# Moving the steps of a depthwise convolution along the taps of a deformable convolution's schedule

## The reference, cut to what matters

```python
# block 0, per image: n = group norm of x
xh = conv1x1(n, w_in, b_in)                     # 64 -> 128 channels
kernels = (relu(mean(xh) @ kg_w1.T + kg_b1) @ kg_w2.T + kg_b2)   # 3x3 taps for each channel
y = depthwise_conv(xh, kernels)
x = x + conv1x1(y * tanh(softplus(y)), w_out, b_out)
# block 1: n = group norm of x
offset, mask = conv3x3(n, w_off), sigmoid(conv3x3(n, w_mask))
xd = sum over 9 taps k of bilinear_sample(n, place k moved by offset) * mask[k], times w_def[:, :, k]
z = conv1x1(concat(xd, offset, mask), w_1x1); batch norm; x = x + silu(z)
```

## Time and profile before

| | us |
|---|---|
| three runs, median (lowest, highest) | 5537.8 (5534.99, 5549.79) |
| the profiled execution | 5550.28 |
| its span, first to last instruction | 5548.3 |
| PE busy | 4469.9 (81%) |
| DVE busy | 4494.7 (81%) |
| ACT busy | 2602.9 (47%) |
| POOL busy | 4053.5 (73%) |

### The profile page before, as it was taken

One profiled execution on the slowest core, in us unless ns is written; L12 is line 12 of the kernel. 1 busy time (PEld: TensorE's weight loads), 2 busy tenths in 40 slices (PEclk: granted clock), 3 DMA queues, 4 the chain that ended last, 5 costly groups with the idle time before them and its releaser, 6 DMA issues.

```text
span 5548.3 us, 46071 instructions
## 1 busy us (share of the span) xinstructions
PE 4469.9 (81%) x14762; PEld 2004.9 (36%) x14762; DVE 4494.7 (81%) x5306; ACT 2602.9 (47%) x3591; POOL 4053.5 (73%) x4243
## 2 busy tenths in 40 slices
PE   7587887887878888788887878788788887888874
PEld 3233333433434333343333433333343343333331
DVE  5888969789797887978889798897978879788765
ACT  4354545445445454444544454454445444445321
POOL 2677777777777777777777777777777777777776
PEclk8688878788787887878888788787878878788896
DMA  4334344353534435344353443435344353433433
GB/s 117 92 118 134 106 132 122 120 132 106 143 106 132 123 112 140 105 131 122 115 137 104 133 123 120 131 105 140 112 130 123 108 143 104 131 116 115 122 108 100
DMA packets 279695, 667.35 MB, mean 120 GB/s; under 512 B 76447, under 2 KB 116762, under 8 KB 277210
## 3 DMA queue, kind: packets, MB, share of 16 engines
q0 software_dynamic: 203328, 555.49, 33.9%
q1 hardware_dynamic: 76128, 108.93, 7.9%
HBM read 610.00 MB, written 54.12 MB: 120 GB/s over the span
## 4 chain that ended last, share of the span: by engine, by line
PE 38%; DVE 27%; POOL 18%; issue 11%; ACT 4%; DMA 2%; DVEq 0%; ACTq 0%; SPq 0%; POOLq 0%
POOL gat L507 18%; PE yo_ps L776 12%; PE tap_ps L776 7%; DVE gat L1370 6%; PE z_ps L698 6%; DVE pairs L1349 5%; DVE conv_ps L1240 5%; DVE hat_s L1397 4%; PE tap_ps L692 3%; PE conv_ps L571 2%; DMA gat<-patch_table,ixu 2%; PE conv_ps L646 2%; PE conv_ps L590 1%; DVE uc L1247 1%; PE xh_ps L758 1%
## 5 line engine op out<-in xcount | busy, mean ns | idle before, releaser
L507 POOL DMA_INDIRECT gat<-patch_table,ixu x4236 | 4045.2, 955 | 1480.6 <-issue 1264.6
L1370 DVE TENSOR_TENSOR gat<-gat,wgt_ps 128x1024 f32<-128x1024 f32 x1059 | 1283.4, 1215 | 445.1 <-DMA gat<-patch_table,ixu 438.1
L1349 DVE TENSOR_REDUCE pairs<-gat 128x256 f32<-128x1024 f32 x1024 | 1239.5, 1210 | 0.0
L776 PE MATMUL yo_ps<-hat_s,hat_image 128*128 128x512 f32 x1860 | 1009.1, 697 | 7.4 <-issue 7.4
L776 PE MATMUL tap_ps<-hat_s,hat_image 128*128 128x512 f32 x1860 | 887.2, 626 | 0.0
L692 PE MATMUL tap_ps<-ident,pairs 128*128 128x128 f32 x2048 | 393.5, 324 | 569.7 <-DVE pairs L1349 569.7
L1040 ACT ACTIVATE val<-tap_ps 128x512 f32<-128x512 f32 x512 | 303.2, 592 | 1094.8 <-PE tap_ps L692 1094.7
L776 PEld LDWEIGHTS yo_ps<-hat_s,hat_image 128*128 128x128 f32 x1860 | 418.5, 233 | 604.5 <-issue 594.5
L1240 DVE SCALAR_TENSOR_TENSOR conv_ps<-xh,kb,conv_ps 128x1024 f32<-128x1024 f32 x480 | 617.4, 1286 | 12.7
L692 PEld LDWEIGHTS tap_ps<-ident,pairs 128*128 128x128 f32 x2048 | 271.8, 163 | 884.0 <-DVE pairs L1349 709.0
L776 PEld LDWEIGHTS tap_ps<-hat_s,hat_image 128*128 128x128 f32 x1860 | 357.4, 201 | 422.2 <-issue 410.1
(11 more groups left out here) (243 smaller groups left out, 4886.5 us busy)
## 6 DMA issues: line engine op xcount, KB each, us to landing
gat<-patch_table,ixu POOLq DMA_INDIRECT x4236, 2.7
xb<-in_x SPq DMA_DIRECT2D x31, 1024.0 KB, 10.4
patch_table<-rec SPq DMA_DIRECT2D x120, 256.0 KB, 2.3
hat_image<-patch_table SPq DMA_DIRECT2D x144, 128.0 KB
out<-n_z SPq DMA_DIRECT2D x128, 128.0 KB, 2.4
patch_table<-np SPq DMA_DIRECT2D x2, 1072.5 KB
patch_table<-gat SPq DMA_DIRECT2D x8, 256.0 KB, 2.2
patch_table<-rec SPq DMA_DIRECT2D x16, 96.0 KB
```

The costliest lines, as they stand in the source:

```text
L507: pool.indirect_dma_start(gat[:, k, t * 2 * REC:(t + 1) * 2 * REC], None, table_rows, bass.IndirectOffsetOnAxis(ixu[:, i, k, t:t + 1], 0)) ...
L776: m = pe.matmul(hat_sums[t % 2][:, :], hat_image[:, q // NCH % 2, i, t, :], hat_s[:, i, :], start=(i == 0), stop=(i == HI - 1))
L1349: dve.tensor_reduce(total, gat[:, k, :].rearrange("p (t x c h) -> p t c x h", t=TILES, x=2, h=2), mybir.AxisListType.XY, ALU.add).then_inc ...
L1370: dve.tensor_tensor(patch, patch, wk.rearrange("p (n h) -> p n h", h=2).unsqueeze(2).to_broadcast([128, TILES * 2, C, 2]), ALU.mult).then_ ...
```

## The change

In every image's chunks 0 to 3 the convolution's rows come one tap earlier, and so do exp, ln and tanh; `project` moves from the next chunk's unit 1 to the own chunk's end, and `residual` from unit 3 to unit 1. The last image has a hat in all its chunks. At the start, the offsets, pixels, indices and points of image 0's chunk 1 come ahead of `hidden(1)`, whose normalisation moves from DVE to ACT. Before tanh, and before the first offsets of an image, ACT loads the set of tables that holds Silu as well as Tanh.

```diff
-PLAN_FIRST = ((2, "convolve 0"), (3, "convolve 1"), (5, "convolve 2"), (6, "exp"), (7, "ln"), (8, "tanh"))
-PLAN_BLOCK0 = ((1, "project"), (3, "residual"), (3, "convolve 0"), (4, "convolve 1"), (5, "convolve 2"), (6, "exp"),
-               (7, "ln"), (8, "tanh"), (8, "finish"))
+PLAN_FIRST = ((1, "convolve 0"), (2, "convolve 1"), (4, "convolve 2"), (5, "exp"), (6, "ln"), (7, "tanh"), (KK, "project"))
+PLAN_BLOCK0 = ((1, "residual"), (2, "convolve 0"), (3, "convolve 1"), (4, "convolve 2"), (5, "exp"), (6, "ln"), (7, "tanh"), (8, "finish"), (KK, "project"))
 PLAN_START = (
...
+    ((2, "first_offsets 2"), (4, "first_offsets 3"), (5, "first_pixels 1"), (6, "first_offsets 4"), (6, "first_points 2"), (8, "first_offsets 5"),
+     (KK, "first_pixels 2")),
+    ((3, "first_offsets 6"), (4, "first_offsets 7"), (5, "first_pixels 3"), (6, "first_points 3")),
+    ((6, "first_points 4"),),
 )
-PLAN_NORM = ((1, "project"), (3, "residual"), (4, "group_mean"), (5, "group_var"), (6, "normalise"), (8, "finish"))
+PLAN_NORM = ((1, "residual"), (4, "group_mean"), (5, "group_var"), (6, "normalise"), (8, "finish"))
...
-    return q < B * NCH and q % NCH in (HATS if q >= NCH else HATS0)
+    return q < B * NCH and (q >= (B - 1) * NCH or q % NCH in (HATS if q >= NCH else HATS0))
...
+    if g < 4:
+        plan = PLAN_BLOCK0 if g > 0 else PLAN_FIRST
+        if b == 0 and g < len(PLAN_START):
+            plan = by_unit(plan, PLAN_START[g])
...
             first_table(7)
+            pe.wait_ge(rec_done, ACT_COPIES[NCH - 1] + REC0)
+            pe.wait_ge(rec_dve, len(BY_DVE))
+            offsets(0, 1, 1)
             x_mean(1)
             x_var(1)
+            first_pixels(0, 1)
             x_norm(1)
             hidden_units(1)
             kernels(1)
...
             for s in range(NCH // 2):
                 hidden(1, s)
-            offsets(0, 1, 1)
-            first_pixels(0, 1)
...
-                steps = {"project": lambda b, g, i: project(b + 1, g - 1),
+                steps = {"project": lambda b, g, i: project(b + 1, g),
...
-                if n > 1:
+                if n > 0:
                     if s == 0:
                         act.wait_ge(kernel_dve, n * KERNEL_STEPS + 7)
...
             def tanh(n, s, buf=0):
                 u = mish[buf]
                 if n > 0:
+                    act.preload_act_table_set("silu_and_others")
...
             def offsets_two(n, s):
 
+                if s == 0:
+                    act.preload_act_table_set("silu_and_others")
...
             x_norm(1)
+            first_points(1)
             kernels(1)
-            for s in range(NCH // 2):
-                hidden(1, s)
-            first_points(1)
```

More of the change, by code:

```diff
@@ L827, in _ @@
             kernels(1)
-            pe.wait_ge(rec_done, ACT_COPIES[NCH - 1] + REC0)
-            pe.wait_ge(rec_dve, len(BY_DVE))
             for s in range(NCH // 2):
                 hidden(1, s)
-            offsets(0, 1, 1)
-            first_pixels(0, 1)
             def image(b, more, further):
-                steps = {"project": lambda b, g, i: project(b + 1, g - 1),
+                steps = {"project": lambda b, g, i: project(b + 1, g),
                          "group_mean": lambda b, g, i: group_mean(b + 1), "group_var": lambda b, g, i: group_var(b + 1),
@@ L1110, in _ @@
             first_index(0)
+            offsets(0, 1, 1)
             x_var(1)
+            first_pixels(0, 1)
             x_norm(1)
             hidden_units(1)
+            first_index(1)
             for s in range(NCH // 2):
                 hidden(1, s)
-            offsets(0, 1, 1)
-            first_pixels(0, 1)
-            first_index(1)
             def image(b, more, further):
@@ L1482, in image @@
                 steps = {"convolve": lambda b, g, i: convolve(b + 1, g, i),
-                         "project": lambda b, g, i: project(b + 1, g - 1),
+                         "project": lambda b, g, i: project(b + 1, g),
                          "residual": lambda b, g, i: residual(b + 1, g - 1), "group_mean": lambda b, g, i: group_mean(b + 1),
```

## The result

The kernel became slower: 5674.9 us (5668.8 to 5682.7, four runs) against 5539.2 (5535.0 to 5549.8, four runs beside them), a ratio of 1.0241 [1.0226, 1.0257]. The forecast was 5680. The profiled execution took 5672.5 us, its span 5670.7.

The account below looks back on a forecast made before the run. POOL's gathers and its waits for the transposes bound the kernel. Profiled 5550.3 + 154 (waits, images 1 to 14) - 3 (image 0) - 11 (last image) = 5690, as a median about 5680 us; range 5590 to 5750.

Parts of the forecast that it names:

- The lever: On POOL, only the number of gathers, its start and its waits for the transposes change the time.
- forecast +154: POOL's added waits over images 1 to 14: +11.0 us an image, +154 us in all.
- The chunk as a chain: Chunks 1 to 3: tap 3 reduced at 26.1, PE's chain 17.3, DVE's end 3.9, so 47.3 us against 44.6.
- The first group: Transposes of the first two taps come about 1 us later, behind residual and first row on DVE; not in the sum.
- I take 17.1 again: PE's chain from group 1's transposes stays 17.1 us, with slow clock after idling, within 13.0 to about 17.8.
- rival C: PE stays at full clock, chain 13.0 us, +0.8 us an image: no change, 5535 us; chance 0.08.
- the bound of 13.0: PE's chain from group 1 at full clock takes 13.0 us, taken from chunk 4.
- the sign that the clock is 0.50 behind both idle stretches: PE idles before group 0 and group 1 in chunks 1 to 3, granted clock 0.50 after both.
- Chunk 0: Tap 3 reduced at 24.9 us; chunk 42.0 or 46.1 us by PE's chain, 43.5 taken, +2.9.
- The product: At the own chunk's end it runs inside DVE's stall, costing nothing; tanh ends near 40.8 us, ahead of 43.4.
- Tables: Silu's own load of 1.28 us goes in some 60 chunks; effect on the time 0.
- the sum (5690): Profiled 5550.3 us + 154 - 3 (image 0) - 11 (last image) = 5690 us.

Follow-up runs that it names:

- the first: Changed kernel with only the convolution's third row put back behind tap 3's reduction in chunks 0 to 3: 5490.3 us, ratio to the kernel before 0.9901.
- second experiment: Kernel before with only the convolution's third row moved ahead of tap 3's reduction: 5777.7 us in one run, against 5549.9.
- third experiment: Kernel before with only product and projection moved to the own chunk's end: 5528.3 us, ratio to the kernel before 0.9966.
- fourth experiment: Kernel before with only image 0's new order, the last image's hats and the Silu-Tanh table set: 5523.3 us, ratio 0.9958.
- sixth experiment: Changed kernel with residual and first row behind tap 1's reduction in chunks 1 to 3: 5674.5 us, ratio to the kernel before 1.0240.
- fifth experiment: Changed kernel plus useless matmuls on PE ahead of groups 0 and 1, chunks 0 to 3 of images 1 to 14: 5628.9 us in one run, against 5546.0.
- the last (5480.2 to 5446.9): Changed kernel, third row behind tap 3, residual and earlier rows behind tap 1 (5480.2 us), plus 8 useless matmuls before group 1: 5446.9 us, ratio 0.9830.

## Why the prediction was right

- **The lever.** Only the number of gathers, POOL's start and its waits for the transposes could change the time. They did: net of issue, the waits of images 1 to 14 went from 73.6 to 226 us, +152 (forecast +154); those of image 0 from 21.4 to 16.3, -5 (-3); the last image's eight gathers fewer are worth 8 x 1.254 = 10 (11). With the shorter gathers (-16, last point) and POOL's first gather (at 104.84 instead of 103.36 us) these make 122, the difference of the spans (5670.7 - 5548.3).
- **The chunk as a chain.** 26.1 + 17.3 + 3.9 = 47.3 was worked out, 26.05 + 17.4 + 3.9 = 47.3 was measured. The third row ahead of tap 3 is shown as the cause from both sides, by the first and the second experiment.
- **Luck in the sum.** That +154 and +152 agree to 2 us is better than the terms do. Over images 1 to 14 chunks 1 and 2 grew by 2.5 and 2.9 us on the mean, close to the 2.7 taken, but chunk 0 by 3.9 (39.9 to 43.8) where 2.9 was taken: 14 us more in all, if POOL waits for all of it as the prediction had it. Against this POOL's waits at tap 0 of chunk 5, 13.0 us net of issue over these images before, are gone after; the prediction counted nothing there for the product that chunk 4 loses. They are gone in the third experiment, which takes that product away too, and still 14.0 in the fourth, which leaves it.
- **The first group.** The second group's lateness sets the sum, so residual and first row ahead of tap 1 cost nothing beside it (sixth experiment). The prediction had counted the second group alone.
- **The clock.** The step "I take 17.1 again" held, and rival C fell: the stretch after 5.65 us of idle was granted 0.50. At full clock the chain measured 13.7 (fifth experiment); the bound of 13.0 was misread from chunk 4, whose chain has no mask matmuls. Of the sign that the clock is 0.50 behind both idle stretches only the half on group 1 came: the 5.8 us from group 0's transposes on (2677.20) were granted 0.69 on the mean. So the clock costs 3.4 us of each such chunk of 47.3; holding it brought 46 us in the fifth experiment (with chunk 0's loss in it) and 33 us, 0.6%, in the last (5480.2 to 5446.9). The Trainium skill (TensorE: Matmul & The Clock Gate, Part 1: The HAM clock gate) puts the ramp penalty at under 1% of a typical kernel's span. What was won back, 0.8% and 0.6% of the total, lies under that, but these are gains from some chunks alone and not the whole cost of the slow stretches. That sentence stands beside the slow matmuls at a kernel's start; the prediction read it as a bound on all slow stretches, and inside the chain that sets a chunk's length the clock costs 7% of the chunk here.
- **Chunk 0.** In image 7 tap 3 came at 24.8 us, forecast 24.9, PE idled 0.98 before its transposes, and the chain was 13.7 at full clock: 42.7 us. Other images went to the upper of the two bounds given (42.0, 46.1), image 4 with 46.1; the mean of 43.8 is near the 43.5 taken.
- **The product.** Costed at nothing, and so it was. Tanh was to end 40.8 us into the chunk, 2.6 ahead of the last hat product; it ended at 40.9, and the hat product began at 43.45. The product waited 1.77 us for tanh (image 7, chunk 2), and that lies inside DVE's stall, of which about 6 us were forecast ahead of the last hat product and 5.71 came, in four places. In the third experiment, where tanh is later, the cover is gone.
- **Tables, last image, projection.** Silu's load (L1050) went from 89 to 29 loads, 114.2 to 37.2 us, and in the fourth experiment, which has the new loads, POOL's waits of images 1 to 14 were no shorter (77.8 us against 73.6). The hats of the last image and image 0's order are the part of the change that helps (fourth experiment, -0.4%).
- **Not foreseen.** POOL's busy time fell by 23.8 us (4053.5 to 4029.7) where eight gathers are 7.6: the mean of a gather went from about 955 to 951 ns. Its long ones, over 1.3 us, are 22 instead of 33, which is a part of it. Over all the kernels run here the mean is 951 to 957 ns. Why was not tested; these 16 us are most of the 17.5 by which the sum (5690) lies above the profiled execution (5672.5).

## What to carry to other kernels

Long work that has no deadline belongs behind the operation that releases an in-order chain on another engine, where it covers the chain; one tap ahead of it, the same 3.8 us delay the chain and uncover it: here that is the difference between 1.0% faster and 2.4% slower. Read the bounding engine's waits by which release ends them, and check every gate on the chain, not only the first: a group made early wins nothing while a later one is late. Moving a tail of steps (exp, ln, tanh, product) forward can be right while moving the row that feeds them is wrong, so try the two apart. Where a sum of terms comes out to 2 us, check the terms one by one: here two errors of 14 and 13 us balanced.

## What the runs showed of the hardware

- Matmuls of no use put into a wait of 5.65 us kept TensorE's granted clock at 1.00 and shortened the chain behind it from 17.1 to 13.7 us; where PE would have idled only 0.98 us, they cost 3.3 us of chunk 0 (fifth experiment, image 7).
- In one execution out of all that were recorded, a record of the hat matmuls took about 2.1 us on the mean instead of 0.7, at a recorded clock of 1.00, and the kernel 14.9 ms; the next four executions of the same kernel took 5.48 to 5.49 ms. The record shows no cause.
